# An attention step on ScalarE: the exponential at the head of the step, ahead of the copies of the turned rows

## The reference, cut to what matters

```python
h = relu(layernorm(x))
# Layer 0: attention over the edges, 4 heads of 32
q, k, v = h @ Wq + bq, h @ Wk + bk, h @ Wv + bv
alpha = einsum('ehc,ehc->eh', q[dst], k[src]) / sqrt(C)
ea = exp(alpha - segment_max(alpha, dst)[dst])
alpha = ea / (segment_sum(ea, dst)[dst] + 1e-16)
x = x + segment_sum(v[src] * alpha[:, :, None], dst) + (h @ Wskip + bskip)
# Layer 1: messages
h = relu(layernorm(x))
h_self, hh = split(h @ W + b)
m = (hh[src] + edge_attr @ We + be) * clip(in_degree[dst], 1)
x = x + h_self + segment_sum(m, dst)
```

## Time and profile before

| | |
|---|---|
| median of 3 runs | 1667.69 us (1666.37 to 1667.74) |
| profiled execution | 1666.32 us, span 1664.6 us |
| TensorE, weight loads | busy 88%, 76% of the span |
| VectorE, ScalarE, GpSimd | busy 78%, 64%, 65% of the span |
| granted TensorE clock, mean | 0.976 of full speed |
| stages, roughly | table to 335 us, attention to 1010 us, messages to the end |

### The profile page before, as it was taken

The page is one execution under the profiler, slowest core; times in us unless marked ns, Lnnn a source line. Parts: engine busy times, 40 slices in busy tenths (PEclk is TensorE's granted clock), DMA queues, the critical chain, the costliest instruction groups (busy, mean ns, idle before and its releaser), DMA issues. The chain is left out here.

```text
span 1664.6 us, 34575 instructions
## 1 busy us (share of the span) xinstructions
PE 1465.6 (88%) x10645; PEld 1262.5 (76%) x10646; DVE 1304.1 (78%) x3599; ACT 1061.2 (64%) x2601; POOL 1075.8 (65%) x1208
## 2 busy tenths in 40 slices
PE   5889888799999999999999983899998999999898
PEld 4667766688888888888888883777776777777676
DVE  8889755288888888888989885677776777777676
ACT  5777877666666666666666641565665665665664
POOL 2565442477777766666666613777777777777774
PEclk9999999899999999999999997999999999999999
DMA  8898897657666666656565615576676676677673
GB/s 215 277 278 295 281 317 244 176 142 191 182 187 183 188 175 177 179 172 180 171 184 166 186 60 141 129 174 166 160 171 148 164 170 165 154 170 163 153 169 98
DMA packets 164789, 303.82 MB, mean 183 GB/s; under 512 B 105752, under 2 KB 109940, under 8 KB 159761
## 3 DMA queue, kind: packets, MB, share of 16 engines
q1 hardware_dynamic: 123740, 202.16, 42.8%
q0 software_dynamic: 40896, 99.90, 23.8%
HBM read 197.23 MB, written 104.50 MB: 181 GB/s over the span
## 5 line engine op out<-in xcount | busy, mean ns | idle before, releaser
L882 POOL DMA_INDIRECT sb_kv<-kv_rows,sb_src_all x500 | 474.8, 950 | 212.5 <-issue 117.3
L910 POOL DMA_INDIRECT sb_kv<-x_rows,sb_src_all x500 | 473.6, 947 | 205.2 <-issue 109.5
L1827 ACT ACTIVATE sb_hn<-sb_xn 100x128 f32<-100x128 f32 x500 | 240.4, 481 | 262.3 <-DMA sb_kv<-x_rows,sb_src_all 226.3
L1830 ACT ACTIVATE sb_vw<-sb_kv 128x128 f32<-128x128 f32 x500 | 239.5, 479 | 0.0
L1739 ACT ACTIVATE sb_hn<-sb_xn,sb_nstat 100x128 f32<-100x128 f32 x500 | 229.5, 490 | 0.0
L1914 PE MATMUL ps_b<-sb_w,sb_memberT 128*125 128x256 f32 x800 | 203.7, 394 | 21.6 <-DVE sb_xn L1000 11.5
L1501 DVE COPY sb_hT<-ps_b 128x400 f32<-128x400 f32 x250 | 142.3, 569 | 95.0 <-PE ps_b L2143 93.5
L1914 PEld LDWEIGHTS ps_b<-sb_w,sb_memberT 128*125 128x125 f32 x800 | 147.8, 195 | 45.6 <-issue 13.6
L2143 PE MATMUL ps_b<-sb_member,sb_vw 128*128 128x100 f32 x1000 | 173.8, 278 | 0.0
L1761 ACT ACTIVATE sb_memberT<-ps_b 100x512 f32<-100x512 f32 x150 | 77.7, 518 | 146.5 <-PE ps_b L2009 143.6
L2143 PEld LDWEIGHTS ps_b<-sb_member,sb_vw 128*128 128x128 f32 x1000 | 157.1, 198 | 10.1 <-issue 10.1
(11 more groups left out here) (202 smaller groups left out, 3116.6 us busy)
## 6 DMA issues: line engine op xcount, KB each, us to landing
kv_rows<-sb_kv SPq DMA_DIRECT2D x26, 1120.0 KB
sb_xn<-x_rows SPq DMA_DIRECT2D x50, 507.8 KB
sb_xn<-in_x SPq DMA_DIRECT2D x50, 500.0 KB
out_rows<-sb_xo SPq DMA_DIRECT2D x49, 500.0 KB
x_rows<-sb_xo SPq DMA_DIRECT2D x24, 1015.6 KB
sb_kv<-in_edge_attr SPq DMA_DIRECT2D x500, 32.0 KB
sb_kv<-in_x SPq DMA_DIRECT2D x28, 560.0 KB
kv_rows<-sb_xn SPq DMA_DIRECT2D x13, 1120.0 KB
```

The costliest lines, as they stand in the source:

```text
L882: pool.indirect_dma_start(out=kvs[:, k % 4, t, :], out_offset=None, in_=kv_rows, in_offset=bass.IndirectOffsetOnAxis(ap=src_all[:, n:n + 1 ...
L910: pool.indirect_dma_start(out=xs1[:, k % 4, t, :], out_offset=None, in_=x1, in_offset=bass.IndirectOffsetOnAxis(ap=src_all[:, n:n + 1], ax ...
L1827: nc.scalar.activation(hn1[:, t, :], xn1[:, k % 4, t, 0:D], ACT.Relu, scale=xn1[:, k % 4, t, D:D + 1], bias=xn1[:, k % 4, t, D + 1:XW]).th ...
L1830: nc.scalar.activation(hs1[:, t, :], xs1[:, k % 4, t, 0:D], ACT.Relu, scale=xs1[:, k % 4, t, D:D + 1], bias=xs1[:, k % 4, t, D + 1:XW]).th ...
```

## The change

In ScalarE's `step0(k)`, `exps(k-1)` is moved from behind the two copies and the first relu to the head of the step. Its wait for `dl` (`A.soft`) moves with it. Nothing else is changed: VectorE's program, which has both first score products ahead of the softmax, is the same in both kernels.

```diff
             def step0(k):
                 nxt = real(k + 1)
+                if real(k - 1):
+                    exps(k - 1)
                 if nxt:
                     copy_h(k + 1, 0)
                     copy_h(k + 1, 1)
                 relus(k + 2, 0, 1)
-                if real(k - 1):
-                    exps(k - 1)
                 if nxt:
                     copy_q(k + 1, 0)
                 relus(k + 2, 1, 3)
```

## The result

The changed kernel takes 1642.69 us (median, 1640.41 to 1648.0) against 1667.15 in the same comparison; the ratio is 0.9858, 95% interval 0.9832 to 0.9884. Its profiled execution took 1644.44 us, span 1642.7, 21.9 us under the span of before. Forecast were 1644.6 us, 23.1 us less than before; the medians differ by 24.5.

The account below looks back on a forecast made before the run. Bound: attention steps, TensorE 91% busy and waiting 1.1 us a step for `wr`. Pairs gain 23 x 1.03 = 23.7 us, step 1 loses 0.6: -23.1 from 1667.69 gives 1644.6 us; own range 1639 to 1652, 8 in 10 1638 to 1658.

Parts of the forecast that it names:

- The bound: Attention stage, TensorE ahead of the transpose in `turn_weights`: waits for softmax weights `wr`, 44.8 us over 40 steps, 1.1 a step.
- Part (a): VectorE's softmax: exponential starts right behind `dl`, so `wr` is ready 1.04 us earlier in plain steps, 0.81 in heavy.
- Part (b): ScalarE's first `hT` copy queues behind the wait for `dl`, delaying TensorE at L1989 0.53 us (plain), 0.76 (heavy).
- rival 1: TensorE's new stall is longer through hand-over and pipeline refilling, about half the gain: 1656 us, chance 0.12.
- The pair: One plain and one heavy attention step: gains 0.61 and 0.42 us, 1.03 of 27.22, in 23 pairs.
- Step 1: Attention stage's step 1, where `dl` comes late: L1989's load 2.03 us later against a `wr` wait of 1.45, 0.58 lost.
- The sum: Whole kernel: 23.7 us gained in steps 2 to 47, 0.6 lost in step 1, -23.1 us in all.
- Rival 2: GpSimd's gathers set the pace, 1.25 us each, 12.5 a step: no change, 1667 us, chance 0.09.
- Rival 3: ScalarE behind a later `dl` holds up copies and TensorE: slower, 1691 us at 1.0 us later, chance 0.08.
- Rival 4: TensorE absorbs the late copy and the whole 1.1 us wait goes: 52 us, 1615 us, chance 0.03.

Follow-up runs that it names:

- the last experiment: Changed kernel with ScalarE's old order (exponential behind both copies and the relu) in the attention stage's step 1 alone: 1649.88 us, ratio 0.9895.

## Why the prediction was right, point by point

- The bound. The wait for `wr` was what the rows had it for: it shrank as the exponential came earlier, place by place (1.12, 0.64, 0.2 and 0 us a step for the exponential behind the relu, behind two copies, behind one, at the head).
- Part (a). Expected was VectorE's wait at 0.3 to 0.4 in a plain step: 0.38. In a heavy step it was to be 0.1 to 0.3 and is nothing; two small instructions cover it.
- Part (b), the term that carried the forecast. Delays of the copy of 0.53 and 0.76 us were worked out. The weight loads of `gather_q` stand right ahead of L1989's on TensorE, first in the kernel before (plain step), then in the changed one (heavy, plain):

```profile
730.89 0.53 PEld L2028 LDWEIGHTS ps_b<-sb_q,sb_memberT 100*128 100x128 f32 x4
```

```profile
704.97 0.53 PEld L2028 LDWEIGHTS ps_b<-sb_q,sb_memberT 100*128 100x128 f32 x4
...
718.26 0.53 PEld L2028 LDWEIGHTS ps_b<-sb_q,sb_memberT 100*128 100x128 f32 x4
```

Before, L1989's load came 731.38 - 730.89 = 0.49 behind them; now it is 719.23 - 718.26 - 0.49 = 0.48 later in the plain step and 706.16 - 704.97 - 0.49 = 0.70 in the heavy one. The hand-over was 0.22 and not 0.24, and the slack of up to 0.05 was there. This also answers rival 1: L1989 comes later by no more than the copy does, and the refilling behind the stall costs 0.05 us: from L1989 to L2039 it is 721.76 - 719.23 = 2.53, and was 735.00 - 1.14 - 731.38 = 2.48 without the wait for `wr`.
- The pair. 1.03 us forecast, 1.06 measured. The heavy step gave the upper end of its 0.38 to 0.47, since `vw` no longer stands behind the third product: it starts 0.30 behind L2039's load (708.99 - 708.69) instead of 0.39. 23 x 1.06 = 24.4.
- Step 1 was mis-sized. 0.58 us lost were forecast; the rows of the step are turned from 335.11 on before and from 334.62 on after (the two rows below), so from there to L2039's load it takes 342.34 - 334.62 = 7.72 us against 340.89 - 335.11 = 5.78, 1.94 lost and not 0.58. The stall itself was met (L1989's load 338.14 against 338.95 forecast, in an execution half a microsecond earlier); what was missing is the lower clock behind it.

```profile
335.11 1.02 PE L1976 MATMUL ps_b<-sb_ident,sb_hn 100*128 100x100 f32 x10
```

```profile
334.62 1.02 PE L1976 MATMUL ps_b<-sb_ident,sb_hn 100*128 100x100 f32 x10
```

- The sum. From the first turn of step 1 to the last turned weights: 666.4 us before, 643.3 after, 23.1 less, the forecast to a tenth. That is closer than its terms, and partly luck: the pairs gave 0.7 us more and step 1 took 1.4 more than forecast, and the last step gave 0.6 (8.41 us from the last but one to the last turned weights, 9.03 before), which the second trace of the changed kernel doesn't have (9.04). The largest term, the pairs, holds in both traces: 26.17 and 26.18 us.
- Rival 2, the gathers: not in a settled step, where 13.08 us a step leave room above 12.5. But in the first five steps they are a bound, and half of the experiments met a wait of 4.7 to 6.4 us for them. Its price of 0.30 us of issue a gather, for which the prediction names rows that don't show it, is in the row above: 116.8 us over 383.
- Rival 3 was the right mechanism to fear, and its threshold (0.6 us in a plain, 0.4 in a heavy step) lies where the runs have it: with `dl` 0.32 us later in every step the changed kernel is still 0.33% ahead of the kernel before, with 0.64 us it is 0.67% behind. Rival 4 is refuted by the relu between the exponential and the copies. Every trace has one load of a function table (1.28 us), ahead of all work at the start of the span, and none in a step.

## What to carry to other kernels

An instruction moved to the head of an in-order engine takes its own wait along, so price two things: what the earlier result gives its reader, and how much later the work behind it starts against the slack of whoever needs that work. Slack is not a property of an instruction: the copy's delay was free while a longer wait stood behind it and cost its full length once that was gone. The better place may be one or two further back: here it is behind the one copy that is just in time, 12 to 14 us faster than at the head of the queue. Or make the awaited value earlier, 19 us, with a move that by itself is worth nothing.

## What the runs showed of the hardware

- A stall of TensorE of 1.7 us cost as much again behind it: from L1989 to L2039 it took 342.34 - 338.14 = 4.20 us, against 708.69 - 706.16 = 2.53 in a later step. The granted clock read 0.72 from 336 to 342 us, 0.51 in the last two of these, and eight matmuls of 128x128 took 1.76 us instead of 1.03 to 1.04. The second trace of the kernel shows the same (0.72, behind a wait of 1.71 us), and so do the three kernels whose copy comes later still in step 1: behind waits of 2.0 to 2.4 us the clock reads 0.50 for some microseconds. The 1.55 us for `wr` in step 1 of the last experiment left the clock at 1.00.
- ScalarE kept two copies whose input was ready behind an exponential whose input wasn't, in the steps shown (the rows were turned by 705.21 us, the copies began at 705.56), and L1989 waited for them in all 40 steps from 400 to 920 us. The Trainium skill, page "TensorE: Matmul & The Clock Gate", section "Architectural detail: the array is 16× 32×32, not 1× 128×128", calls the queues of ScalarE and VectorE strictly first in, first out; the trace agrees, with L1989's wait of 0.44 to 0.67 us.
- A scan of 0.40 us costs 0.32 us of VectorE's time when the instruction behind it doesn't depend on it; a pair of settled steps grew by 0.62 us with one scan a step and by 1.25 with two.
- Single executions scatter by some microseconds for a reason outside the change: GpSimd's first gather starts between 305.2 and 310.7 us in the traces, though nothing ahead of it differs between the kernels. The ratios of medians of four are known to 0.2 to 0.3%.
